# Segment sums as two float32r passes, and a state-space loop with its turn and output one place sooner

## The reference, cut to what matters

```
proj = hidden @ in_proj_w.T               # gate, xBC, dt
xBC  = silu(causal_conv4(xBC));  dt = softplus(dt + dt_bias);  A = -exp(A_log)
dA   = dt * A                             # per token and head
L    = exp(segsum(dA))                    # per chunk: exp of sums dA[s+1..t], t >= s
Y_diag = einsum(C, B, L, x*dt)            # inside a chunk
states = einsum(B, exp(dA_cum[-1]-dA_cum), x*dt)
Y_off  = einsum(C, states carried over chunks, exp(dA_cum))
hg   = (Y_diag + Y_off + D*x) * silu(gate)
out  = (hg * rsqrt(mean(hg^2) + eps) * norm_w) @ out_proj_w.T ;  x = x + out
```

## Time and profile before

| | us |
|---|---|
| median of 3 runs | 716.97 (716.85 to 722.58) |
| profiled execution, its own time | 719.14 |
| its span | 717.3 |
| the loop over tiles, first tokens to last output | 375.8 to 507.4 of the span |

### The profile page before, as it was taken

How to read it: one execution, slowest core, us unless ns; L and a number is a source line. 1 busy time by engine, 2 the same in 40 slices (tenths; PEclk the granted TensorE clock), 3 DMA queues, 4 the chain that set the end, 5 groups by cost and what they waited for, 6 DMA issues and landing times.

```text
span 717.3 us, 13912 instructions
## 1 busy us (share of the span) xinstructions
PE 557.5 (78%) x5668; PEld 403.4 (56%) x5668; DVE 405.2 (56%) x597; ACT 370.4 (52%) x791; POOL 147.3 (21%) x115
## 2 busy tenths in 40 slices
PE   0187868577967686668999999998639999999980
PEld 0044546454545571345564556666528999997560
DVE  5889998868899367883755545453461121111223
ACT  6986887457786615754557555644321222222212
POOL 1000000000000125841009555520010322322210
PEclk9995687785597999988999999998758999999996
DMA  9500000000000100000000000000049999889825
GB/s 354 163 1 1 1 1 1 1 0 1 1 1 1 30 1 1 0 1 1 1 3 2 2 3 2 3 2 2 31 164 383 422 419 379 307 329 339 309 124 190
DMA packets 18479, 71.38 MB, mean 100 GB/s; under 512 B 4848, under 2 KB 9968, under 8 KB 14704
## 3 DMA queue, kind: packets, MB, share of 16 engines
q1 hardware_dynamic: 15408, 64.20, 23.6%
q0 software_dynamic: 1920, 5.25, 2.0%
q10 hardware_dynamic: 1088, 1.05, 0.4%
HBM read 65.77 MB, written 4.72 MB: 98 GB/s over the span
## 4 chain that ended last, share of the span: by engine, by line
PE 56%; DVE 26%; ACT 10%; issue 4%; DMA 2%; POOL 1%; SPq 0%; ACTq 0%; DVEq 0%; POOLq 0%
PE PS L1416 41%; DVE nmx L1017 3%; DVE arena L930 3%; DVE arena L927 3%; PE PS L1891 2%; PE PS L1454 2%; PE PS L1960 2%; ACT arena L604 1%; PE PS L1667 1%; DVE A L949 1%; PE PS L1532 1%; ACT arena L764 1%; DVE arena L1121 1%; PE PS L1492 1%; DMA arena<-ypair 1%
## 5 line engine op out<-in xcount | busy, mean ns | idle before, releaser
L1416 PE MATMUL PS<-arena 128*128 128x128 f32 (+6 forms) x1376 | 162.1, 296 | 17.1 <-DVE arena L1121 10.1
L1416 PEld LDWEIGHTS PS<-arena 128*128 128x128 f32 (+4 forms) x1376 | 129.3, 167 | 43.0 <-issue 26.1
L604 ACT ACTIVATE arena<-PS,nmx 128x128 f32<-128x128 f32 (+1 forms) x128 | 52.1, 424 | 44.8 <-DVE nmx L1017 44.8
L1469 PE MATMUL PS<-ident,arena 128*128 128x128 f32 x192 | 37.6, 350 | 32.6 <-ACT arena L591 30.5
L1364 DVE TENSOR_TENSOR R<-arena,PS 128x128 f32<-128x128 f32 x16 | 4.6, 288 | 89.3 <-ACT arena L858 89.2
L1469 PEld LDWEIGHTS PS<-ident,arena 128*128 128x128 f32 x192 | 29.1, 181 | 40.4 <-ACT arena L604 25.7
L383 POOL TENSOR_SCALAR arena<-ident,gcol 128x128 f32<-128x128 f32 x4 | 2.4, 601 | 234.0 <-DMA gcol<-in_gcol 234.0
L443 POOL TENSOR_TENSOR arena<-arena 128x1024 f32<-128x1024 f32 x16 | 37.8, 2367 | 41.1 <-DVE arena L1203 33.1
L475 POOL DMA_INDIRECT ypair<-arena,oid x20 | 19.8, 988 | 122.5 <-ACT arena L864 122.5
L1416 PE MATMUL PS<-arena,R 128*128 128x256 f32 x192 | 44.2, 380 | 0.6 <-ACT arena L864 0.6
L1416 PEld LDWEIGHTS PS<-arena,R 128*128 128x128 f32 x192 | 35.2, 190 | 5.1 <-issue 1.0
(11 more groups left out here) (299 smaller groups left out, 1202.9 us busy)
## 6 DMA issues: line engine op xcount, KB each, us to landing
arena<-in_moe SPq DMA_DIRECT2D x23, 1408.0 KB, 6.6
arena<-in_moe SPq DMA_DIRECT2D x23, 768.0 KB
inproj<-in_inproj SPq DMA_DIRECT2D x1, 1344.0 KB, 10.5
arena<-in_fT SPq DMA_DIRECT2D x1, 1024.0 KB, 4.9
xT<-in_xT SPq DMA_DIRECT2D x1, 1024.0 KB, 5.4
R<-in_w1T SPq DMA_DIRECT2D x1, 1024.0 KB, 7.4
R<-in_w2T SPq DMA_DIRECT2D x1, 1024.0 KB, 9.4
R<-in_w3T SPq DMA_DIRECT2D x1, 1024.0 KB, 11.5
```

The lines of the kernel that those rows point to most:

```text
L604: sc.activation(pr[u % 2][:, j, 0:n], PS[:, 2 * (u % 2) + j // 2, (j % 2) * 256:(j % 2) * 256 + n], ACT.Exp, bias=nmx[:, u % 2, j:j + 1], ...
L1416: last = mm(dst, l, r, start=(n == 0), stop=(n == len(pairs) - 1))
L1469: last = nc.tensor.transpose(PSB[:, 4 * HALF + c:4 * HALF + c + P], pr[u % 2][:, j, k * P:(k + 1) * P], ident[:])
```

## The change

1. `dA` is split on DVE into a float32r copy `dAh` (rounded by the write) and the remainder `dAl` (two more instructions after L1174, `dve_dt` now counts to 2, and POOL and PE wait for 2).
2. `ugt` and `gtf` get float32r copies (two ACT copies of 128 x 128; PE waits for `act_opw` at 6 before the decay sums).
3. Each segment sum and each of the four `gtf` sums is now two float32r matmuls (high, low) that accumulate, in place of one in float32.
4. POOL's `steps(i)` builds the 2048 high columns and then 1024 low ones (`lower[..][0]`); DVE's new `lower_steps(i)` the other 1024 (`lower[..][1]`, `dve_stp`). The last is placed ahead of the loop for tiles 0 and 1, and in iteration i between gated(i-1) and add_out for tile i + 2.
5. PE's and ACT's loops are reordered. turn(i-1) goes behind state(i, 1), output(i-1) behind state(i, 3), the first two segment sums to the front, tokens(i+1) behind state 4. DVE's add_out(i-1) stands in iteration i in place of add_out(i-2).

```
+            done(v.tensor_copy(dAh[:], dA), "dve_dt")
+            done(v.tensor_tensor(dAl[:], dA, dAh[:].bitcast(F), ALU.subtract), "dve_dt")
+            def lower_steps(i):
+                if i >= 2:
+                    dve.wait_ge(S["pe_seg"], 4 * (i - 1))
+                each = [P, SH // 2, Q]
+                done(v.tensor_tensor(lower[i % 2][1][:], dAl[:, i, 32:64].bitcast(F).unsqueeze(2).broadcast_to(each),
+                                     step[:].unsqueeze(1).broadcast_to(each), ALU.mult), "dve_stp")
...
             for i in range(NT):
                 if i:
                     gated(i - 1)
-                if i >= 2:
-                    add_out(i - 2)
+                if i + 2 < NT:
+                    lower_steps(i + 2)
+                if i:
+                    add_out(i - 1)
                 if i + 1 < NT:
                     front(i + 1)
...
             def tokens(i):
-                if 1 <= i <= 2:
-                    pe.wait_ge(S["dve_xw"], i)
-                    pe.wait_ge(S["dve_tok"], i)
-                if i >= 3:
-                    pe.wait_ge(S["act_hgt"], i - 2)
-                    pe.wait_ge(S["dve_x"], X_FFN + i - 2)
+                if i == 1:
+                    pe.wait_ge(S["dve_xw"], 1)
+                    pe.wait_ge(S["dve_tok"], 1)
+                if i >= 2:
+                    pe.wait_ge(S["act_hgt"], i - 1)
+                    pe.wait_ge(S["dve_x"], X_FFN + i - 1)
...
             def segments(i, q):
-                pe.wait_ge(S["pool_stp"], i + 1)
+                pe.wait_ge(S["pool_stp"], 2 * i + 2)
+                if q >= 2:
+                    pe.wait_ge(S["dve_stp"], i + 1)
...
             for i in range(NT):
-                state(i, 1)
                 if i + 1 < NT:
                     segments(i + 1, 0)
                     segments(i + 1, 1)
-                    tokens(i + 1)
+                state(i, 1)
+                if i:
+                    turn(i - 1)
                 state(i, 2)
                 state(i, 3)
+                if i:
+                    output(i - 1)
                 if i + 1 < NT:
                     segments(i + 1, 2)
                     segments(i + 1, 3)
                 if i % 2 == 0:
                     state(i, 4)
+                if i + 1 < NT:
+                    tokens(i + 1)
                 within(i)
-                if i:
-                    turn(i - 1)
                 between(i)
-                if i:
-                    output(i - 1)
```

More of the change, by code:

```diff
@@ L76, in at, with next_at, placed @@
             return v
+        def next_at():
+            return (nc.sbuf_base + 31) // 32 * 32
+        def placed(name, at, words, shape, dt):
+            return nc.alloc_sbuf_tensor_at(name, shape, dt, offset=at + 4 * words)
         xT = sb("xT", [P, CT, N])
+        A_at = next_at()
         A = sb("A", [P, CT, N])
+        R_at = next_at()
         R = sb("R", [P, 4, NCH, CT * HALF])
@@ L95, in build @@
         wu = sb("wu", [P, 4, 2, CT])
+        inproj_at = next_at()
         inproj = sb("inproj", [P, CT, PROJ])
@@ L134, in build @@
         sums = [arena[:, w:w + K] for w in range(8 * K, 12 * K, K)]
-        ekq, ekvq = arena[:, 12 * K:13 * K], sb("ekvq", [P, N])
+        ekq = arena[:, 12 * K:13 * K]
+        ekvq_at = next_at()
+        ekvq = sb("ekvq", [P, N])
         tiny = sb("tiny", [P, 2])
+        dmats_at = next_at()
         dmats = [sb(f"dmat{i}", [P, N]) for i in range(2)]
@@ L184, in build @@
         lm = [wide(0), wide(2 * K)]
-        stp = [wide(4 * K), spent[:, 512:512 + 2 * K].rearrange("p (h t) -> p h t", h=SH)]
+        stp = [placed(f"stp{i}", at, w, [P, SH, Q], FR) for i, (at, w) in enumerate(((arena_at, 4 * K), (inproj_at, 512)))]
         xbd = [wide(12 * K + 512).rearrange("p h (c q) -> p h c q", c=NC), wide(14 * K + 512).rearrange("p h (c q) -> p h c q", c=NC)]
+        lower = [[placed(f"lower{i}{l}", at, l * K, [P, SH // 2, Q], FR) for l in range(2)] for i, at in enumerate((dmats_at, A_at))]
+        dAh = placed("dAh", ekvq_at, 512, [P, NT, SH], FR)
+        dAl = placed("dAl", R_at, 2 * 2 * K + 3 * 512, [P, NT, SH], FR)
+        ugtr = placed("ugtr", arena_at, 29 * K + 512, [P, P], FR)
+        gtfr = placed("gtfr", arena_at, 29 * K + 512 + P, [P, P], FR)
         es = arena[:, 6 * K:6 * K + 512].rearrange("p (c i h) -> p c i h", c=NC, i=NT)
@@ L206, in build @@
         anegb = sb("anegb", [P, SH])
-        def placed(name, words, shape, dt):
-            return nc.alloc_sbuf_tensor_at(name, shape, dt, offset=arena_at + 4 * words)
         ring = arena[:, 0:RING * EW].rearrange("p (r n) -> p r n", r=RING)
@@ L289, in build @@
             act_hgt act_rs dve_dec act_decay pool_pad dve_rinv pe_r act_rT dve_num act_ekq act_ekvq act_sq act_yw
-            dve_hqt dve_iden dve_msq dve_peak pe_rows pe_ss pool_diag pool_osc pool_root dve_ht pe_ht""".split()
+            dve_hqt dve_iden dve_msq dve_peak pe_rows pe_ss pool_diag pool_osc pool_root dve_ht pe_ht dve_stp""".split()
         S = {n: sem(n) for n in NAMES}
@@ L434, in steps @@
                     pool.wait_ge(S["pe_seg"], 4 * (i - 1))
-                pool.tensor_tensor(stp[i % 2], dA[:, i, :].unsqueeze(2).broadcast_to([P, SH, Q]),
+                pool.tensor_tensor(stp[i % 2][:], dAh[:, i, :].bitcast(F).unsqueeze(2).broadcast_to([P, SH, Q]),
                                    step[:].unsqueeze(1).broadcast_to([P, SH, Q]), ALU.mult).then_inc(S["pool_stp"], 1)
+                each = [P, SH // 2, Q]
+                pool.tensor_tensor(lower[i % 2][0][:], dAl[:, i, 0:32].bitcast(F).unsqueeze(2).broadcast_to(each),
+                                   step[:].unsqueeze(1).broadcast_to(each), ALU.mult).then_inc(S["pool_stp"], 1)
             def masked_decay(i, half):
@@ L448, in _ @@
             last.then_inc(S["pool_diag"], 1)
-            pool.wait_ge(S["dve_dt"], 1)
+            pool.wait_ge(S["dve_dt"], 2)
             steps(0)
@@ L694, in _ @@
                 sc.activation(outproj[:, k, :], outproj[:, k, :], ACT.Copy, scale=normw[:, k:k + 1]).then_inc(S["act_opw"], 1)
+            sc.activation(ugtr[:], ugt[:], ACT.Copy).then_inc(S["act_opw"], 1)
+            sc.activation(gtfr[:], gtf[:], ACT.Copy).then_inc(S["act_opw"], 1)
             act.wait_ge(S["dve_dtx"], 1)
@@ L792, in _ @@
                     decays(i + 1, 1)
+                state(i, 1)
+                if i:
+                    turned(i - 1)
                 state(i, 2)
                 state(i, 3)
+                if i:
+                    inverse_root(i - 1)
                 if i + 1 < NT:
@@ L801, in _ @@
                     by_chunk(i + 1)
-                if i:
-                    turned(i - 1)
-                    inverse_root(i - 1)
                 if i == NT - 2:
@@ L1173, in _ @@
             done(v.scalar_tensor_tensor(dt, dt, 0.0, ut.rearrange("p (i h) -> p i h", i=NT), ALU.max, ALU.add))
-            done(v.tensor_tensor(dA, dt, anegb[:].unsqueeze(1).broadcast_to([P, NT, SH]), ALU.mult), "dve_dt")
+            done(v.tensor_tensor(dA, dt, anegb[:].unsqueeze(1).broadcast_to([P, NT, SH]), ALU.mult))
+            done(v.tensor_copy(dAh[:], dA), "dve_dt")
[3 more added lines that the diff above has]
+                    dve.wait_ge(S["pe_seg"], 4 * (i - 1))
+                each = [P, SH // 2, Q]
+                done(v.tensor_tensor(lower[i % 2][1][:], dAl[:, i, 32:64].bitcast(F).unsqueeze(2).broadcast_to(each),
+                                     step[:].unsqueeze(1).broadcast_to(each), ALU.mult), "dve_stp")
+            lower_steps(0)
             for n in range(6):
@@ L1248, in _ @@
             dve.wait_ge(S["act_gate"], NT)
+            lower_steps(1)
             for i in range(NT):
@@ L1257, in _ @@
             gated(NT - 1)
-            add_out(NT - 2)
             b48 = [P, 4, NE]
@@ L1646, in decay_sum @@
                     m = Q * (n + 1)
-                    last = acc(PS[0:m, b, :], [(gtf[0:m, 0:m], dA[0:m].rearrange("p i h -> p (i h)"))])
+                    last = acc(PS[0:m, b, :], [(gtfr[0:m, 0:m], w[0:m].rearrange("p i h -> p (i h)")) for w in (dAh, dAl)])
                 else:
@@ L1672, in _ @@
                 conv_in(n)
-            pe.wait_ge(S["dve_dt"], 1)
+            pe.wait_ge(S["act_opw"], XT + 2)
+            pe.wait_ge(S["dve_dt"], 2)
             for n in range(NC + 2):
@@ L1707, in segments @@
                     pe.wait_ge(S["act_seg"], 4 * i + q - 1)
-                acc(bank(q % 2), [(ugt[:], stp[i % 2][:, 16 * q:16 * q + 16, :].rearrange("p h t -> p (h t)"))], "pe_seg")
+                acc(bank(q % 2), [(ugtr[:], w.rearrange("p h t -> p (h t)")) for w in
+                                  (stp[i % 2][:, 16 * q:16 * q + 16, :], lower[i % 2][q // 2][:, 16 * (q % 2):16 * (q % 2) + 16, :])],
+                    "pe_seg")
             def state(i, c):
@@ L1762, in turn @@
                 pe.wait_ge(S["dve_hg"], i + 1)
-                pe.wait_ge(S["dve_xw"], min(i + 3, NT))
```

(7 more changed lines are left out.)

1 line of the change is left out of this document (removed).

## The result

| | before | after |
|---|---|---|
| median of 5 runs each, us | 716.97 | 739.92 (738.49 to 743.26) |
| profiled execution / its span, us | 719.14 / 717.3 | 743.26 / 741.4 |
| ratio of the runs | | 1.0305 (95%: 1.0258 to 1.0352) |
| tokens(0) to ACT behind output(7), span us | 375.8 to 507.4: 131.6 | 376.5 to 530.5: 154.0 |

What follows compares the result with a forecast made beforehand. PE bounded the loop; the new closed round of waits would replace it. Stretches +9.9, +7.0, -9.9, before the loop -1.1, clock +6.0: 719.14 + 11.9 = 731.0, forecast 729 since the profiled run was 2.2 above median; range 711 to 738.

Steps and rivals of the forecast that it cites:

- What bounds it, and the cycle: Loop: a closed round of waits through DVE, ACT and PE replaces PE's work; two tiles take 34.1 us against 30.2.
- The port: DVE's gated instructions with both inputs in SBUF wait for POOL; odd tiles take 20.0 us, undisturbed 15.8.
- float32r: Segment sums: two passes, at most 0.24 us each, make 0.45 from 0.85; decay sums before the loop save 1.1.
- The clock: PE's granted clock falls behind its 6.2 us pauses before turn in tiles 1 and 3: +6.0 us, bounds 0 and 9.
- The last stretch: From tokens(7) to the end of output(7): 25.2 us in place of 35.1, -9.9.
- the first stretch: From tokens(0) to tokens(2): ends at 405.2 against 395.31, +9.9 us, with 14.1 plus 3.4 after tokens(1).
- the forecast loop (+13.0): Loop over tiles: the three stretches together +7.0 us, and the clock +6.0.
- The rivals: Five other outcomes: 720 us (0.18), 711 or 708 (0.17), 736 to 742 (0.12), 748 (0.04), unchanged 717 (0.03).
- The case of two more falls (736 to 742): POOL wins the port at each boundary, L1228 waits 3.4 us in tiles 2 and 4: 736, up to 742; chance 0.12.
- The range: Whole kernel: 711 to 738 us, leaving out the last of the fast case and the float32 rate.

Runs made afterwards that it cites:

- e3_pool_waits: Changed kernel, but POOL waits for gated(i-1) before steps(i+2); 736.1 us, ratio 1.0213.
- e5_wait_warm: e3_pool_waits plus short unused matmuls in PE's pauses (before tile 1's first sums, each turn, even tiles' tokens); 726.4 us, ratio 1.0099.
- e12_order_wait_warm: e1_order (float32 sums) plus POOL's wait for gated and unused matmuls before each turn and the first state 3; 727.2 us, ratio 1.0133.
- e6_before_warm: Kernel before plus 16 unused matmuls in its loop's one long PE pause, ahead of the last state 3; 716.7 us, ratio 0.9934.
- e4_warm: Changed kernel plus unused matmuls ahead of each turn: 30 before turn(1) and turn(3), 6 before the others; 744.8 us, ratio 1.0339.
- e1_order: Kernel before with only the new order of PE, ACT and DVE, sums still float32; 735.9 us, ratio 1.0213.

## Why the forecast was right and wrong

The loop grew by 22.3 us. Two experiments divide it, by the loop's length in one trace of each: e3_pool_waits takes 148.8, e5_wait_warm 138.6, the kernel before 131.6. So freeing the port is worth 5.1 us, filling the pauses 10.2, and 7.0 remain with the order, the fillings' own cost and one fall. By the ratios, which rest on all executions, the three parts are some 6.6, 8.2 and 7.1 us, each uncertain by several. They depend on the sequence in which they are taken away.

Where the 7.0 lie in e5_wait_warm says what the cycle itself costs. tokens(0) to tokens(2) takes 33.3 us in place of 19.3 (with the one fall in it), tokens(2) to tokens(7) 79.7 in place of 77.0, and the rest 25.6 in place of 35.3. Of the 79.7, 3.7 are pauses of PE with no release in the profile (1.62 of the 77.0). So with the port free and the clock up, the round of waits in the middle tiles is about as long as PE's work was before. It is no loss by itself there; it takes away what the sums save, and the start of the loop pays.

- **What bounds it, and the cycle: right.** The new chain is the one that was worked out, and PE's 13 us bring nothing clear in it: with the port and most of the clock mended, the split sums have 1.0099 (e5_wait_warm) and the float32 ones 1.0133 (e12_order_wait_warm), with intervals that overlap. Even tiles were forecast at 14.1 us and take 14.25 (393.01 to 407.25 and 430.46 to 444.71 from tokens to tokens).
- **The port: right, even in size.** Forecast for odd tiles: L1234 and L1235 end at 12.7 us after tokens; the trace has 444.71 to 457.50, 12.8. e3_pool_waits shows the cause.
- **float32r: right,** 0.23 a pass of the 0.24 taken as a bound, and 1.0 us before the loop of 1.1.
- **The clock: the step that failed,** "I count a fall for each, 3.0 twice": +6.0 in the sum, where the trace has some 17.7 (an estimate: 4.7 for the first fall, 3.1 each for those at turn(1) and turn(3), 3.3 at turn(5), 3.5 for the last two). The price was right for three falls: 10.4 us (turn(1), turn(3)) and 10.6 (turn(5)) against 7.3 from turn to tokens, and 3.0 in e6_before_warm. The count was wrong, two for six, because I let the clock fall only behind pauses like the one in the earlier trace rows, and I read that one as 4 us. It was 2.97, as the first row here, of before, shows. The others, of after, are falls that I didn't count:

```profile
489.88 1.22 PE L1416 MATMUL PS<-R,arena 96*128 96x512 f32 x1 [2.97 <-ACT arena L756]
...
382.29 0.79 PE L1451 MATMUL PS<-stp,ugtr 128*128 128x512 f32 x1 [1.76 <-POOL lower L452]
491.24 0.99 PE L1805 MATMUL PS<-ident,arena 128*128 128x128 f32 x4 [1.30 <-DVE arena L1268]
508.71 1.12 PE L1805 MATMUL PS<-ident,arena 128*128 128x128 f32 x4 [1.27 <-DVE arena L1261]
524.38 0.66 PE L1805 MATMUL PS<-ident,arena 128*128 128x128 f32 x4 [1.59 <-DVE arena L1268]
```

From tokens(0) to tokens(1) the first of them made 16.5 us of a forecast 11.8; e5_wait_warm, with this pause filled, takes 11.7, so this fall alone cost 4.7. Tile 5, without POOL's steps beside it and forecast at 15.8, took 19.6 (482.22 to 501.82): 3.3 by the clock and 0.5 by a pause of PE of 0.90 with no release (485.55). The last stretch, with two falls, took 28.7 in place of 25.2. Those three are 4.7 + 3.8 + 3.5 = 12.0 us. Against them the first stretch saved 3.2, since tile 1, being late, met POOL less (14.25 in place of 17.5). The sum of both, +8.8, is most of the 9.3 us between the forecast loop (+13.0) and the measured one.

- **The rivals.** None was it. The case of two more falls (736 to 742) has the measured time but laid it to POOL winning the port at each boundary. In the profiled run L1261 waited 0.3 in each even tile, so DVE won there, and so it did at every other such boundary (last section).
- **The range** left out the falls behind short pauses, though I had pauses of 1 to 2 us in the other tiles of the new cycle. With bounds of 0 and 18 us for the clock it would have held the time; 18 is what the trace has, known only afterwards.

## What to carry to other kernels

Here an order that puts its engines one behind the other once a tile was paid twice: the round of waits took away what the shorter matmuls saved, and the matmul engine stood a little in each round and fell to half clock. Before matrix work is shortened at the cost of steps on DVE and POOL, work out the round of waits through the other engines; and look which of DVE's instructions with both inputs in SBUF would run beside POOL's. Where a pause can't be had out, a few unused matmuls in it may be worth more than they cost, as 3 us in the kernel before; in e4_warm, where they outlasted the pause, they were not.

## What the runs showed of the hardware that was not expected

- Pauses of 1.3 us ahead of turn were enough to go with a fall of the granted clock (491.24, 508.71), while others of 1.2 (399.92, 437.39, 474.89) were not; in e3_pool_waits one of 1.18 was (467.01), and in e1_order the clock fell at 398 with only 0.41 us of standing ahead of turn (396.36). What divides them is not settled: those at 491 and 508 had further pauses of 0.9 us shortly before (485.55, 506.33). Unused matmuls in the pauses removed most falls (e5_wait_warm), which shows the bond with PE standing.
- POOL's steps took 4.67 us in e3_pool_waits (416.33) in place of 3.64, with one low step of DVE before them, and two masks 6.63 in place of 4.70 in the changed kernel: the port blocks POOL as well.
- At the boundary of two POOL instructions that followed each other at once, a DVE instruction that already waited went first: eight times of eight in the trace of the changed kernel between 399 and 479, with POOL's next instruction the longer for it (3.95 at 399.42 and 474.39, 3.97 at 436.86, in place of 3.64). What made L1261 wait 2.6 us in e4_warm (436.07) was that it came 0.8 after such a boundary.
- PE stood 0.9 to 2.1 us inside within or between with nothing the profile shows as its release, once in the trace of before, twice in that of after, up to six times in those with fillings. It was not pursued.
